# Cross-attention: the float32 quarter in every second head only, the other last quarters split by VectorE

## The chip, the cores and the metric

The kernel runs on one core of a Trainium2 chip. The metric is device time in microseconds, from one launch of the whole program; lower is better.

## The reference

The program is a two-layer block over x (4 x 512 x 512, float32) with a context of 4 x 1024 x 512: a gated masked cross-attention, a top-1 mixture of eight ternary experts, a second gated cross-attention with 16 heads, and a dense expert layer. The change lies in the second cross-attention alone:

```python
Q = query @ Wq.T + bq                      # 4 x 512 x 512, 16 heads of 32
K = key_value @ Wk.T + bk                  # 4 x 1024 x 512
V = key_value @ Wv.T + bv
scores = jnp.einsum('bhsd,bhtd->bhst', Q, K) * scale
attn = jax.nn.softmax(scores, axis=-1)     # over 1024 keys
ctx = jnp.einsum('bhst,bhtd->bhsd', attn, V)
return ctx @ Wo.T + bo
```

## The kernel before, in words

The phases run one after the other: context, readout, router, mixture, queries, **attention** (`attention_phase`, about 729 to 1180 us of the profile), output, experts. Attention walks over 64 heads (4 batches of 16), and each head over four quarters u = 0 to 3 of its 1024 keys, so there are 256 steps (h, u). Float32 accuracy comes from pairs of bf16 numbers: a high half and a low half.

In step (h, u) each engine does, in the order in which its queue is written:

- **TensorE** (PE): at one step in sixteen `max_transpose` (L1903); then `max_scores` (L1894) for the quarter of queries 28 steps ahead, four matmuls into one of two places of psM; then `scores` (L1916), four matmuls for the quarter of keys four steps ahead, into psE; then `mix` for the current quarter, into psO. The mix of quarters 0 to 2 is six bf16 matmuls (L1930): three products of the halves of the weights (the high half is read in place as the upper 16 bits of the float32 exponential, `upper`) and of the values, on two sides of the array at once. The mix of quarter 3 (`FULL = (3,)`) takes the float32 exponentials and float32 values directly: two float32 matmuls (L1935), which stand in the trace as four records.
- **VectorE** (DVE): `halves` for the quarter three steps ahead (L1819; only quarter 0 of the last seven heads), then `maximum` (L1811), the reduction of the psM place that the max_scores of this step fill; at u = 1 of every fourth head `next_values` joins the two halves of the next batch's values to float32 (L1603, `t_v`). At a few places it does odd work (bias split, sums and their reciprocal L1852 and L1854 at head 56).
- **ScalarE** (ACT): two exponentials (L1773) from psE into a ring of eight float32 quarters `t_e32`, four steps ahead; after quarter 3 the copy of psO (L1787).
- **GpSimd** (POOL): `halves` for the quarter four steps ahead: low = e32 - upper(e32) (L1726, `t_low`) for quarters 0 to 2; at one step in sixteen four small operations on the maxima (`max_parts`, L1736 to L1742).
- **SyncE** issues the loads and stores.

`wait_free` sets when max_scores may write a place of psM: the reduction of the max_scores two places before must be done. The transposed rows (L1903) take a place of their own in step (2, 1) of each group of four heads, so the max_scores that follow them there wait for the reduction of the step directly before, that of step (2, 0). The low halves lie in six slots, three for even and three for odd heads.

```python
for _, h, u in steps(b):                       # VectorE
    b2, h2, u2 = ahead(b, h, u, AHEAD - 1)
    if within(b2, h2):
        halves(b2, h2, u2)
    b2, h2, u2 = ahead(b, h, u, EARLY)
    if within(b2, h2):
        maximum(b2, h2, u2)
    prepare_output(b, h, u)
    if u == 1:
        next_values(b * NH + h - G - 3)
```

Of the kernel before, what the change touches and what calls it, by code (L numbers as in the profile page):

```python
# [7 lines left out]
BF16 = mybir.dt.bfloat16  # L8
# [4 lines left out]
P = 128  # L13
B, S, D = 4, 512, 512
T = 1024
KC = D // P
NH, HD = 16, 32
# [1494 lines left out]
def attention_phase(nc, queries_dram, keys_dram, values_dram, mixed_dram, sums_dram, ident, qst, loaded, kst, vst, kv_loaded, ones_set, o):  # L1512
# [7 lines left out]
    G = HG  # L1520
    TC = T // P
    AHEAD, MAXAHEAD = 4, 7
    RING = 8
    FULL = (3,)
    SIDE = P // 2
    NLD = 3
    mixed_v = mixed_dram.rearrange("b r (h d) s -> b h r d s", h=NH)
# [2 lines left out]
    with ExitStack() as c:  # L1530
        sb = lambda name, shape, dt: c.enter_context(nc.sbuf_tensor(name, shape, dt))
        sem = lambda name: c.enter_context(nc.semaphore(name))
        e32 = sb("t_e32", [P, RING, 2, S], F32)
        low = sb("t_low", [P, RING - 2 * len(FULL), 2, S], BF16)
        v32 = sb("t_v32", [P, G, TC, VW * G], F32)
        nmax = sb("t_nmax", [P, 2, G, 4], F32)
        nrest = sb("t_nrest", [P, G, 4], F32)
# [21 lines left out]
        mixed, mix_cleared, sums_added = sem("t_mixed"), sem("t_mix_cleared"), sem("t_sums_added")  # L1559
        copied_out = sem("t_copied_out")  # L1560
        stored = [sem(f"t_stored{i}") for i in range(2)]

        def on_pool(head, u):

            return u not in FULL and not on_dve(head, u)

        def on_dve(head, u):

            return u == 0 and head >= B * NH - MAXAHEAD

        def upto(chosen, head, u):

# [2 lines left out]
        def wait_lo(eng, head, u):  # L1575

            if on_pool(head, u):
                eng.wait_ge(lo_pool, upto(on_pool, head, u))
            else:
                eng.wait_ge(lo_dve, upto(on_dve, head, u))  # L1580

        def slot(h, u):

            return (h * 4 + u) % RING

        def low_slot(h, u):

            return h % 2 * (4 - len(FULL)) + u

        def upper(h, u):  # L1590

            return e32[:, slot(h, u), :, :].rearrange("p i s -> p (i s)").bitcast(BF16).rearrange(
                "p (i s w) -> p i s w", i=2, w=2)[:, :, :, 1]

        def ahead(b, h, u, n):

            h, u = h + (u + n) // 4, (u + n) % 4
            return b + h // NH, h % NH, u

        def join_values(engine, b, g):  # L1600

            halves = [vst[:, g, :, r * VW * G:r * VW * G + P] for r in range(2)]
            return engine.tensor_tensor(v32[:, g, :, 0:P], halves[0], halves[1], ALU.add).then_inc(v32_ready[g], 1)  # L1603

        def steps(b):
            return [(b, h, u) for h in range(NH) for u in range(4)]
# [7 lines left out]
        def within(b, h):  # L1614

            return not (isinstance(b, int) and b > LAST)
# [30 lines left out]
        def group_at(b, h, u, step):  # L1647

            if (4 * h + u) % GROUP == step:
                b2, h2, _ = ahead(b, h // G * G, 0, GROUP)  # L1650
                if within(b2, h2):
                    return b2, h2 // G
            return None

        with nc.Block() as block:
# [64 lines left out]
            @block.gpsimd  # L1720
            def _(pool):
                def halves(b, h, u):
                    head = b * NH + h
                    if on_pool(head, u):
                        pool.wait_ge(expd, head * 8 + 2 * u + 2)
                        nc.gpsimd.tensor_tensor(low[:, low_slot(h, u), :, :], e32[:, slot(h, u), :, :], upper(h, u),  # L1726
                                                ALU.subtract).then_inc(lo_pool, 1)

                def max_parts(b, g):

                    k = b * G + g
                    pool.wait_ge(maxed, k * GROUP + GROUP)
                    if not (isinstance(b, int) and b == 0 and g == 0):
                        pool.wait_ge(n_xposed, k)
                    m, zeros = nmax[:, g % 2, :, :], nparts[:, 3, :, :]
                    nc.gpsimd.tensor_tensor(nparts[:, 0, :, :], m, zeros, ALU.subtract).then_inc(n1_done, 1)  # L1736
                    pool.wait_ge(n1_done, k + 1)
                    nc.gpsimd.tensor_tensor(nrest[:, :, :], m, nparts[:, 0, :, :], ALU.subtract).then_inc(nrest_done, 1)
                    pool.wait_ge(nrest_done, k + 1)
                    nc.gpsimd.tensor_tensor(nparts[:, 1, :, :], nrest[:, :, :], zeros, ALU.subtract).then_inc(n2_done, 1)  # L1740
                    pool.wait_ge(n2_done, k + 1)
                    nc.gpsimd.tensor_tensor(nparts[:, 2, :, :], nrest[:, :, :], nparts[:, 1, :, :],  # L1742
                                            ALU.subtract).then_inc(n3_done, 1)

                nc.gpsimd.memset(nparts[:, :, :, :], 0.0).then_inc(zeros_set, 1)
                pool.wait_ge(zeros_set, 1)
                nc.gpsimd.memset(o.bones[:, :], 1.0).then_inc(o.bones_set, 1)
                pool.wait_ge(zeros_set, 1)
                nc.gpsimd.memset(v32[:, :, :, P:], 1.0).then_inc(v32_ones, 1)
                for g in range(G):  # L1750
                    pool.wait_ge(kv_loaded[g], 16 * KV_LOADS)
                    join_values(nc.gpsimd, 0, g)
                max_parts(0, 0)
                for n in range(AHEAD):
                    halves(*ahead(0, 0, 0, n))
                def batch(b):
                    for _, h, u in steps(b):
                        b2, h2, u2 = ahead(b, h, u, AHEAD)
                        if within(b2, h2):
                            halves(b2, h2, u2)  # L1760
                        if due := group_at(b, h, u, SPLIT_AT):
                            max_parts(*due)
                for b in range(B):
                    batch(b)
# [42 lines left out]
            def _(dve):  # L1807
# [7 lines left out]
                def halves(b, h, u):  # L1815
                    head = b * NH + h
                    if on_dve(head, u):
                        dve.wait_ge(expd, head * 8 + 2 * u + 2)
                        nc.vector.tensor_tensor(low[:, low_slot(h, u), :, :], e32[:, slot(h, u), :, :], upper(h, u),  # L1819
                                                ALU.subtract).then_inc(lo_dve, 1)  # L1820

                nc.vector.memset(psO[:, :, :], 0.0).then_inc(mix_cleared, 1)
                for m in range(EARLY):
                    maximum(*ahead(0, 0, 0, m))
                    if m >= EARLY - AHEAD + 1:
                        halves(*ahead(0, 0, 0, m - EARLY + AHEAD - 1))
# [56 lines left out]
            def _(pe):  # L1883
# [36 lines left out]
                def mix(b, h, u):  # L1920

                    head = b * NH + h
                    g = h // G
                    high, whole = upper(h, u), e32[:, slot(h, u), :, :]

                    def values(i, r):
                        return vst[:, g, 2 * u + i, r * VW * G:(r + 1) * VW * G].rearrange("p (w h) -> p h w", h=G)[:, h % G, :]

                    def add(side, i, r, part, first=False, last=False):
                        return nc.tensor.matmul(psO[side * SIDE:side * SIDE + VW, h % 2, :], values(i, r), part[:, i, :],  # L1930
                                                start=first, stop=last)

                    def add_whole(i, last):
                        v = v32[:, g, 2 * u + i, :].rearrange("p (w h) -> p h w", h=G)[:, h % G, :]
                        return nc.tensor.matmul(psO[i * SIDE:i * SIDE + VW, h % 2, :], v, whole[:, i, :], start=False, stop=last)  # L1935

                    if u in FULL:
                        pe.wait_ge(expd, head * 8 + 2 * u + 2)
                        if h % G == 0:
                            pe.wait_ge(v32_ready[g], b + 1)  # L1940
                        add_whole(0, u == 3)
                        add_whole(1, u == 3).then_inc(mixed, 1)
                        return
                    if u == 0:
                        pe.wait_ge(copied_out, head + 1)
                    rest = low[:, low_slot(h, u), :, :]
                    wait_lo(pe, head, u)
                    add(0, 0, 0, high, first=u == 0)
                    add(1, 0, 0, rest, first=u == 0)
                    add(0, 1, 0, high)  # L1950
                    add(1, 1, 0, rest)
                    add(0, 0, 1, high, last=u == 3)
                    add(1, 1, 1, high, last=u == 3).then_inc(mixed, 1)
# [627 lines left out]
```

## Time and profile before

| what | value |
|---|---|
| median of 3 runs | 1642.63 us (1638.8 to 1645.27) |
| the profiled execution's own time | 1641.37 us |
| its span | 1639.6 us |
| granted TensorE clock, mean over the span | 0.922 |
| busy over the span: PE, DVE, ACT, POOL | 86%, 69%, 58%, 32% |
| busy in 800 to 900 us, inside attention: PE, DVE, ACT, POOL | 99.8, 82.7, 75.3, 93.6 us of 100 |
| L1726, GpSimd's subtraction | 185 times, 2.0 us in the mean |
| L1811, VectorE's reduction | 256 times, 1.22 us |

The shares over the whole span mix phases with different limits; the row of 800 to 900 us is what bears on the change. Times are microseconds unless marked ns. PE is the matmul side of TensorE, PEld its weight loads, which overlap it. A line of the timeline gives start, duration (of the whole run of instructions where several are merged, marked x2, x3 and so on), engine, line, operation and tiles, and in brackets the idle time before it with what ended it. The clock is a share of 2.4 GHz; the chip grants either all or half of it.

### The profile page before, as it was taken

To read this page: it belongs to the slowest core of one execution; us is meant where nothing else is said; L and a number is where in the kernel's file an instruction comes from. 1 tells how busy PE (TensorE), PEld (TensorE's weight loads), DVE (VectorE), ACT (ScalarE), POOL (GpSimd) and SP (SyncE) were. 2 spreads that over 40 slices of the span, in tenths; PEclk is the share of its full clock that TensorE was granted. 3 is DMA by queue.
4 is the path that set the end of the run, shared out by engine and by line. 5 is a ranking of instruction groups with operands and counts; after the bars stand their busy time and mean duration, and the time that the engine had idled before them with its cause. 6 is when DMAs were issued, how large, how long until landed. Compare 5 with 4: busy or idle time off the path is not lost. (4 is left out here: it accounts for less than half of the span.)

```text
span 1639.6 us, 26673 instructions
## 1 busy us (share of the span) xinstructions
PE 1409.4 (86%) x9883; PEld 851.5 (52%) x9959; DVE 1132.4 (69%) x1444; ACT 950.4 (58%) x1440; POOL 524.4 (32%) x401
## 2 busy tenths in 40 slices
PE   4999996999942794779999999999795899999996
PEld 3555453555422352323776776775233666666663
DVE  4788856578873596838778788786576676565561
ACT  5788843445433595423777777777623866665651
POOL 0122210000053005314999999997520000000000
PEclk8999998999965896876999999999897899999998
DMA  6688761000028438430353443542481876656640
GB/s 232 222 288 305 249 218 40 1 1 1 1 81 342 136 125 204 107 90 4 67 105 85 86 98 71 104 113 81 99 287 52 295 255 231 207 204 211 220 145 27
DMA packets 162674, 233.22 MB, mean 142 GB/s; under 512 B 46396, under 2 KB 80191, under 8 KB 161416
## 3 DMA queue, kind: packets, MB, share of 16 engines
q1 hardware_dynamic: 157064, 206.60, 41.8%
q0 software_dynamic: 5504, 25.20, 4.2%
q8 instruction: 67, 1.10, 0.3%
q14 instruction: 39, 0.32, 0.1%
HBM read 169.62 MB, written 55.65 MB: 137 GB/s over the span
## 5 line engine op out<-in xcount | busy, mean ns | idle before, releaser
L1726 POOL TENSOR_TENSOR t_low<-t_e 128x1024 bf16<-128x1024 f32 x185 | 365.0, 2001 | 48.1 <-ACT t_e L1773 48.1
L1811 DVE TENSOR_REDUCE t_nmax<-t_psM 128x1 f32<-128x1024 f32 x256 | 309.5, 1221 | 75.0 <-PE t_psM L1894 73.6
L1773 ACT ACTIVATE t_e<-t_psE 128x512 f32<-128x512 f32 x512 | 277.9, 595 | 105.0 <-PE t_psE L1916 97.5
L1894 PE MATMUL t_psM<-kst,qst 96*64 96x512 bf16 x1024 | 189.0, 406 | 14.0 <-DVE t_nmax L1811 7.0
L2411 PE MATMUL e_psG<-late_flat,e_w1p 128*128 (+1 forms) x1536 | 172.3, 275 | 13.7 <-DVE e_hT L2355 9.1
L1916 PE MATMUL t_psE<-qst,kst 99*64 99x512 bf16 x1024 | 181.9, 386 | 1.3
L2411 PEld LDWEIGHTS e_psG<-late_flat,e_w1p 128*128 128x128 bf16 x1536 | 151.3, 99 | 35.2 <-issue 8.3
L1930 PE MATMUL t_psO<-t_e,vst 128*33 128x512 bf16 x768 | 163.9, 392 | 3.7 <-POOL t_low L1726 3.7
L2426 PE MATMUL e_psO<-e_w2p,e_hT 128*128 128x512 bf16 x752 | 164.9, 379 | 0.8
L1894 PEld LDWEIGHTS t_psM<-kst,qst 96*64 96x64 bf16 x1024 | 89.0, 113 | 77.8 <-DVE t_nmax L1811 35.0
L2426 PEld LDWEIGHTS e_psO<-e_w2p,e_hT 128*128 128x128 bf16 x768 | 75.0, 98 | 89.0
L1930 PE MATMUL t_psO<-t_low,vst 128*33 128x512 bf16 x384 | 115.0, 380 | 0.0
L1916 PEld LDWEIGHTS t_psE<-qst,kst 99*64 99x64 bf16 x1024 | 80.6, 108 | 58.9 <-ACT t_e L1773 44.7
L116 POOL DMA_DIRECT2D ternary<-c_wout x48 | 42.5, 886 | 179.9 <-ACT c_wout L228 179.9
L2307 ACT CAST e_w2p<-xres 128x2048 bf16<-128x2048 f32 x32 | 60.7, 1898 | 52.7 <-PE e_psO L2426 27.2
L2313 ACT ACTIVATE e_g<-e_psG,e_b1T 128x256 f32<-128x256 f32 x128 | 53.5, 469 | 64.0 <-PE e_psG L2411 36.8
L1930 PEld LDWEIGHTS t_psO<-t_e,vst 128*33 128x33 bf16 x768 | 76.5, 109 | 23.7 <-POOL t_low L1726 4.7
L675 PE MATMUL a_psS<-ctxT,a_xT 128*128 128x512 bf16 x373 | 86.4, 386 | 0.7 <-issue 0.2
L358 PE MATMUL c_psG<-ctxT,c_wT 128*128 128x512 bf16 x369 | 85.7, 379 | 0.8
L361 PE MATMUL c_psG<-c_wT,ctxT 128*128 128x512 bf16 x371 | 85.6, 379 | 0.7
L2347 DVE TENSOR_TENSOR e_w1p<-piece,e_w1p 128x2048 bf16<-128x2048 f32 x32 | 72.2, 2287 | 18.2 <-ACT e_w1p L2302 18.2
L2355 DVE TENSOR_TENSOR e_hT<-e_g,e_hT 128x512 bf16<-128x512 f32 x64 | 43.7, 689 | 51.0 <-ACT e_hT L2316 51.0
(268 smaller groups left out, 2376.4 us busy)
## 6 DMA issues: line engine op xcount, KB each, us to landing
piece<-in_L_ffn_w SPq DMA_DIRECT2D x32, 1024.0 KB, 13.8
xres<-in_L_ffn_w SPq DMA_DIRECT2D x32, 1024.0 KB, 14.8
wT<-ternary POOLq DMA_DIRECT2D x8, 1536.0 KB
kst<-keys SPq DMA_DIRECT2D x96, 128.0 KB, 3.5
c_rows<-in_ctx SPq DMA_DIRECT2D x8, 1024.0 KB, 9.4
xres<-in_L_ffn_wg SPq DMA_DIRECT2D x8, 1024.0 KB, 6.1
xres<-in_L_ffn_wu SPq DMA_DIRECT2D x8, 1024.0 KB, 6.8
xres<-in_L_ffn_wd SPq DMA_DIRECT2D x8, 1024.0 KB, 6.2
```

The source lines that it names most:

```text
L358: last = nc.tensor.matmul(psG[:, k, :], wT[:, 0, a, k * P:(k + 1) * P], ctxT[:, b, q * 512:(q + 1) * 512], start=(i == 0), stop=(i == 11))
L361: last = nc.tensor.matmul(psG[:, k, :], ctxT[:, a, q * 512 + k * P:q * 512 + (k + 1) * P], wT[:, 1, b, :], start=(i == 0), stop=(i == 11))
L675: last = nc.tensor.matmul(psS[:, par, h * 512:(h + 1) * 512], xT[:, par, ra * KC + k, :], ctxT[:, rb * KC + k, bass.ds(b * T + h * 512, 512)],
L1726: nc.gpsimd.tensor_tensor(low[:, low_slot(h, u), :, :], e32[:, slot(h, u), :, :], upper(h, u), ALU.subtract).then_inc(lo_pool, 1)
L1773: nc.scalar.activation(e32[:, slot(h, u), i, :], psE[:, i, :], ACT.Exp, scale=SC).then_inc(expd, 1)
L1811: nc.vector.tensor_reduce(nmax[:, h // G % 2, h % G, u:u + 1], banks_of(place_of_max(b, m)).rearrange("p a t -> p (a t)"), AX_X, ALU.max, ...
L1894: last = nc.tensor.matmul(banks_of(place_of_max(b, m))[side * SIDE:(side + 1) * SIDE, i, :], qst[0:KR, g, h % G, s0:s0 + SIDE], kst[0:KR, ...
L1916: last = nc.tensor.matmul(psE[side * SIDE:(side + 1) * SIDE, i, :], kst[:, g, h % G, t0:t0 + SIDE], qst[:, g, h % G, :], start=True, stop= ...
L1930: return nc.tensor.matmul(psO[side * SIDE:side * SIDE + VW, h % 2, :], values(i, r), part[:, i, :], start=first, stop=last)
L2347: nc.vector.tensor_tensor(half1(1, p), raw1(p), half1(0, p), ALU.subtract).then_inc(w1_lo, 1)
L2411: last = nc.tensor.matmul(psG[:, g % 4, i, :], w1p[:, ra, k, f:f + P], xeT[:, rb * KC + k, ee, :].rearrange("p o s -> p (o s)"), start=(n ...
L2426: last = nc.tensor.matmul(psO[:, m, :], hT[:, ra, k, m * P:(m + 1) * P], w2p[:, rb, k, :], start=(k == 0 and i == 0), stop=(k == FC - 1 an ...
```

## The change

In heads with an odd number the last quarter stays float32 (`is_whole`). In even heads it becomes a bf16 quarter like the other three: its low half is formed by VectorE (`on_dve`), in the VectorE step (h, 0) of the same head, ahead of that step's reduction. The low slots become one ring of six over the seven low quarters of each pair of heads, and each engine that forms a low half first waits until the mix that read the slot before is done (`wait_low_free`). TensorE's wait for the joined values moves from the first to the second head of each group of four. GpSimd still forms three low halves for each head.

```diff
-    FULL = (3,)
+    LOWS = 6
...
-        low = sb("t_low", [P, RING - 2 * len(FULL), 2, S], BF16)
+        low = sb("t_low", [P, LOWS, 2, S], BF16)
...
+        def is_whole(head, u):
+            return u == 3 and head % 2 == 1
+
         def on_pool(head, u):
-            return u not in FULL and not on_dve(head, u)
+            return not is_whole(head, u) and not on_dve(head, u)

         def on_dve(head, u):
-            return u == 0 and head >= B * NH - MAXAHEAD
+            return u == 3 and head % 2 == 0 or u == 0 and head >= B * NH - MAXAHEAD
+
+        def low_count(head, u):
+            return head // 2 * 7 + head % 2 * 4 + u
+
+        def wait_low_free(eng, head, u):
+            n = low_count(head, u) - LOWS
+            if n >= 0:
+                pair, quarter = divmod(n, 7)
+                eng.wait_ge(mixed, pair * 8 + quarter + 1 + RING)
...
-        def low_slot(h, u):
-            return h % 2 * (4 - len(FULL)) + u
+        def low_slot(head, u):
+            return low_count(head, u) % LOWS
...
                 def halves(b, h, u):                      # GpSimd; VectorE the same with on_dve
                     head = b * NH + h
                     if on_pool(head, u):
+                        wait_low_free(pool, head, u)
                         pool.wait_ge(expd, head * 8 + 2 * u + 2)
...
-                    if u in FULL:
+                    if is_whole(head, u):
                         pe.wait_ge(expd, head * 8 + 2 * u + 2)
-                        if h % G == 0:
+                        if h % G == 1:
                             pe.wait_ge(v32_ready[g], b + 1)
```

## Rows read from the trace of the kernel before

**Rows 1.** Busy time of each engine in one group of four heads.
```profile
core 0: us, PE busy (x) PEld busy (x) DVE busy (x) ACT busy (x) POOL busy (x), PEclk, DMA share, GB/s
921.21:947.21 26.00, 25.95 (x221) 18.59 (x218) 20.95 (x18) 19.64 (x38) 24.10 (x17) 1.00 0.43 88
```

**Rows 2.** Groups by line, 735 to 1230 us: busy, mean ns, idle before, releaser.
```profile
L1811 DVE TENSOR_REDUCE t_nmax<-t_psM 128x1 f32<-128x1024 f32 x252 | 304.8, 1221 | 73.7 <-PE t_psM L1894 72.4
...
L1935 PE MATMUL t_psO<-t_e,t_v 128*33 128x512 f32 x256 | 72.0, 598 | 0.0
...
L1603 DVE TENSOR_TENSOR t_v<-vst 128x1024 f32<-128x1024 bf16 x12 | 20.6, 1714 | 0.0
L1819 DVE TENSOR_TENSOR t_low<-t_e 128x1024 bf16<-128x1024 f32 x7 | 9.1, 1293 | 23.3 <-ACT t_e L1773 23.3
```

**Rows 3.** Timeline of TensorE, steps (1, 2) to (2, 1) of heads 20 to 23.
```profile
904.95 0.38 PE L1930 MATMUL t_psO<-t_low,vst 128*33 128x512 bf16 x1
...
905.61 0.75 PE L1894 MATMUL t_psM<-kst,qst 96*64 96x512 bf16 x4
...
906.51 1.15 PE L1935 MATMUL t_psO<-t_e,t_v 128*33 128x512 f32 x4
907.37 0.72 PE L1894 MATMUL t_psM<-kst,qst 96*64 96x512 bf16 x4
...
909.14 0.23 PE L1903 MATMUL t_psM<-ident,t_nparts 128*128 128x128 bf16 x1
909.42 0.62 PE L1894 MATMUL t_psM<-kst,qst 96*64 96x512 bf16 x4
```

**Rows 4.** Timeline of ScalarE, VectorE and GpSimd in the same steps.
```profile
906.69 1.08 ACT L1773 ACTIVATE t_e<-t_psE 128x512 f32<-128x512 f32 x2 [0.47 <-PE t_psE L1916]
...
908.14 1.22 DVE L1811 TENSOR_REDUCE t_nmax<-t_psM 128x1 f32<-128x1024 f32 x1 [0.50 <-PE t_psM L1894]
...
906.87 0.22 POOL L1736 TENSOR_TENSOR t_nparts<-t_nmax,t_nparts 128x16 bf16<-128x16 f32 x1
...
907.76 0.21 POOL L1742 TENSOR_TENSOR t_nparts<-t_nrest,t_nparts 128x16 bf16<-128x16 f32 x1
907.93 1.89 POOL L1726 TENSOR_TENSOR t_low<-t_e 128x1024 bf16<-128x1024 f32 x1
```

**Rows 5.** Timeline of all three around the join before head 24.
```profile
917.63 1.71 DVE L1603 TENSOR_TENSOR t_v<-vst 128x1024 f32<-128x1024 bf16 x1
...
919.26 1.21 DVE L1811 TENSOR_REDUCE t_nmax<-t_psM 128x1 f32<-128x1024 f32 x1
...
920.40 2.34 DVE L1811 TENSOR_REDUCE t_nmax<-t_psM 128x1 f32<-128x1024 f32 x2
...
916.37 1.89 POOL L1726 TENSOR_TENSOR t_low<-t_e 128x1024 bf16<-128x1024 f32 x1 [0.99 <-ACT t_e L1773]
...
918.22 2.87 POOL L1726 TENSOR_TENSOR t_low<-t_e 128x1024 bf16<-128x1024 f32 x1
...
921.05 1.89 POOL L1726 TENSOR_TENSOR t_low<-t_e 128x1024 bf16<-128x1024 f32 x1
...
922.91 1.89 POOL L1726 TENSOR_TENSOR t_low<-t_e 128x1024 bf16<-128x1024 f32 x1
...
918.81 0.75 PE L1894 MATMUL t_psM<-kst,qst 96*64 96x512 bf16 x4
...
920.56 0.73 PE L1894 MATMUL t_psM<-kst,qst 96*64 96x512 bf16 x4
...
923.66 0.59 PE L1894 MATMUL t_psM<-kst,qst 96*64 96x512 bf16 x3
```

**Rows 6.** Timeline of GpSimd, VectorE and TensorE at head 56.
```profile
1132.17 5.02 POOL L1726 TENSOR_TENSOR t_low<-t_e 128x1024 bf16<-128x1024 f32 x1 [2.37 <-ACT t_e L1773]
...
1134.29 1.15 DVE L1819 TENSOR_TENSOR t_low<-t_e 128x1024 bf16<-128x1024 f32 x1
1135.37 2.33 DVE L1811 TENSOR_REDUCE t_nmax<-t_psM 128x1 f32<-128x1024 f32 x2
...
1136.63 0.62 PE L1894 MATMUL t_psM<-kst,qst 96*64 96x512 bf16 x4 [3.27 <-DVE t_nmax L1811]
```

**Rows 7.** Busy time and granted clock of the 4 us after that stall.
```profile
1138.00:1142.00 4.00, 4.00 (x22) 1.48 (x20) 2.06 (x2) 2.69 (x6) 1.05 (x1) 0.57 0.21 51
```

More of the change, by code:

```diff
@@ L1724, in halves @@
                     if on_pool(head, u):
+                        wait_low_free(pool, head, u)
                         pool.wait_ge(expd, head * 8 + 2 * u + 2)
-                        nc.gpsimd.tensor_tensor(low[:, low_slot(h, u), :, :], e32[:, slot(h, u), :, :], upper(h, u),
+                        nc.gpsimd.tensor_tensor(low[:, low_slot(head, u), :, :], e32[:, slot(h, u), :, :], upper(h, u),
                                                 ALU.subtract).then_inc(lo_pool, 1)
@@ L1817, in halves @@
                     if on_dve(head, u):
+                        wait_low_free(dve, head, u)
                         dve.wait_ge(expd, head * 8 + 2 * u + 2)
-                        nc.vector.tensor_tensor(low[:, low_slot(h, u), :, :], e32[:, slot(h, u), :, :], upper(h, u),
+                        nc.vector.tensor_tensor(low[:, low_slot(head, u), :, :], e32[:, slot(h, u), :, :], upper(h, u),
                                                 ALU.subtract).then_inc(lo_dve, 1)
@@ L1945, in mix @@
                         pe.wait_ge(copied_out, head + 1)
-                    rest = low[:, low_slot(h, u), :, :]
+                    rest = low[:, low_slot(head, u), :, :]
                     wait_lo(pe, head, u)
```

## The prediction, made before the run

> **What bounds the kernel now.** I read the busy times by stretch first, then the groups of instructions by line, then the timeline of one group of four heads. In the stretch of four heads of [rows 1] TensorE is busy 25.95 of 26.00 us at full clock, GpSimd 24.10, VectorE 20.95, ScalarE 19.64. So TensorE sets the pace of attention, GpSimd is 1.9 us behind it, and a shorter TensorE step can be worth something. [Rows 3] show the steps from the start of one kind of matmul to the next: the mix of a bf16 quarter takes 904.95 to 905.61, 0.66 us, that of the float32 quarter 906.51 to 907.37, 0.86 us.
>
> "Busy" hides how little room the other engines have. TensorE's max_scores write two buffers of psM that VectorE must reduce before they are written again. As a rule that leaves two steps, but where the transposed rows (L1903) take one of the two places, the next max_scores waits for the reduction directly before it. [Rows 3, 4] show this: the reduction that starts at 908.14 ends at 909.36, and the max_scores start at 909.42. That is 0.06 us after it, with no room at all, once in every four heads.
>
> **What the change removes.** In 32 of 64 heads the float32 mix (0.86 us) becomes a bf16 mix (0.66 us): 32 x 0.20 = 6.4 us less on TensorE [rows 3]. The range of this term is 5 to 6.4 us, since ScalarE is nearly as slow as a bf16 step (a pair of exponentials plus its wait is 1.08 + 0.47 = 1.55 us, [rows 4]), and since the last heads are not paced by TensorE.
>
> **What it adds.** 32 subtractions on VectorE. The same instruction stands in the trace seven times, near the end, at 1.29 us in the mean [rows 2]; back to back the next VectorE instruction starts 1.08 us after it (1134.29 to 1135.37, [rows 6]). In VectorE's queue the subtraction for quarter 3 of an even head h stands in step (h, 0), right in front of the reduction of that step. So not VectorE's total matters (20.95 + 2 x 1.3 = 23.6 of 26), but how late that one reduction becomes. Nothing is added to GpSimd's own count (three a head, as before); its new wait for a free low slot is for a mix of six or seven quarters earlier, while the exponentials that it waits for anyway come out at most four quarters ahead of the mix. So it costs nothing, and the ring of six is no limit.
>
> **The port.** [Rows 5] show what a VectorE instruction with two SBUF inputs and a GpSimd subtraction do to each other. The join of the values is issued at 917.63, while GpSimd works until its next one starts at 918.22. VectorE's next instruction starts at 919.26, so the join held something for 1.04 us after 918.22 and had waited 0.59 before. GpSimd's subtraction of 918.22 takes 2.87 us and not 1.89: it stood still for 0.98. In [rows 6] a GpSimd subtraction that starts at 1132.17 takes 5.02 us, over a reciprocal and the added subtraction after it: VectorE got its second turn though GpSimd was waiting. I take it that each added subtraction waits for the GpSimd instruction under way, is then next, and takes 1.05 us from both.
>
> The Trainium skill states this rule (SBUF — State Buffer, "Who interferes with whom"): a VectorE instruction with two SBUF inputs and a GpSimd instruction that reads SBUF exclude each other, and the second to issue blocks fully until the first is done. That speaks against this change, as the added work is of just that kind; the join's row agrees, and without the rule the forecast would be the third rival below.
>
> GpSimd's budget by this: 12 x 1.85 (918.22 would follow 916.37 by 1.85) + 1.06 for the maxima's parts (906.87 to 907.93, [rows 4]) + 0.98 for the join = 24.2 us in four heads; with two blocks of 1 us, 26.2. That is just over the old period of 26.0 and under the period that comes out below, so it does not bind.
>
> **Heads 2, 6, ... 54 (14 times), step (2, 0).** The exponentials of quarter 3 end at 907.77 (906.69 + 1.08, [rows 4]), so the subtraction is ready at 907.84. GpSimd is then in the last small part (from 907.76), and its next large one starts at 907.93. VectorE goes first: 907.93 + 1.05 = 908.98 is the start of the reduction, + 1.22 = 910.20 its end, + 0.06 = 910.26 the max_scores, which started at 909.42. Stall 0.84 us; 14 x 0.84 = 11.8 us. The margin to GpSimd's start at 907.93 is only 0.09 us: were GpSimd first, the stall would be 1.85 more.
>
> **Heads 0, 4, ... 56, step (0, 0).** In [rows 5] VectorE comes out of the join late: its last reduction before the step starts at 920.40 and the next thing could start at 921.53. The exponentials are there by then (0.40 after the max_scores of 920.56, as 907.77 after 907.37). GpSimd is in the subtraction that started at 921.05 and hands over at 922.91. The added subtraction holds until 923.96, the reduction ends at 925.17, and the max_scores of step (0, 2), now at 923.66, start at 925.23. Stall 1.57 us, at 12 heads (12 joins, [rows 2]): 18.8 us. Where no join precedes (heads 0, 4 and 56), GpSimd is 0.98 earlier and hands over at 921.93: reduction ended 924.19, stall 0.6. At head 56 the sums and the reciprocal follow this reduction, and the whole delay of 0.65 + 1 adds to the stall that is there [rows 6]: 1.6. Together 0.6 + 0.6 + 1.6 = 2.8 us.
>
> In the new frame GpSimd still idles about 1 us before quarter (2, 0) and 0.6 before (0, 0), so it starts each pair on time, and these phases repeat in each group.
>
> **Sum.** 11.8 + 18.8 + 2.8 - 6.4 = +27.0 us. The profiled execution took 1641.37 us, which gives 1668.4; from the median of the runs, 1642.63, it is 1669.6. I say 1670. In four heads: 26.0 - 0.4 + 0.84 + 1.57 = 28.0 us.
>
> Bounds of the added stalls: from below nothing (only -6.4 us, 1636); from above, if GpSimd is first at the 14 close places, 14 x 1.85 = 26 us more, 1696.
>
> **Rivals.**
> A. *The subtraction is hidden* and the change does what it takes off TensorE: 1642.6 - 6.4 = 1636. For it: the join, 1.71 us of VectorE, moved TensorE by nothing; the step behind it is 1.75 us (918.81 to 920.56, [rows 5]) as it is elsewhere (905.61 to 907.37, [rows 3]). Against it: the reduction two steps on ended at 920.47 and the max_scores started at 920.56 [rows 5], so the join uses up all the room, and at 909.42 there was none. It decides if VectorE gets to the subtraction over 1.2 us before the reduction's data. Chance 0.04.
> B. *GpSimd first at the close places*: the stall of 0.84 becomes 2.69. 1696. For it: a margin of 0.09 us. Against: VectorE got the turn at both contested places of rows 5 and 6. Chance 0.13.
> C. *No exclusion at the port*, or GpSimd out of phase: then the subtraction costs only VectorE's time. At (2, 0): 907.84 + 1.13 + 1.22 + 0.06 = 910.25, stall 0.83; at (0, 0) after a join: 921.53 + 1.13 + 1.21 + 0.06 = 923.93, stall 0.27; at the others none but 1.1 at head 56. 11.6 + 3.2 + 1.1 - 6.4 = +9.5, 1652. Against: 2.87 and 5.02 us of rows 5 and 6. Chance 0.11.
> D. *The clock*: after the one long stall of TensorE (3.27 us before 1136.63, [rows 6]) the granted clock was 0.57 in the 4 us from 1138 [rows 7], that is mostly the 1.2 GHz level. If a stall of 1.6 us did that 12 times, some 3.4 us at half speed each cost 1.7: 12 x 1.7 = 20 us more, 1690. Against: the pause here is half as long. Chance 0.12.
> E. *GpSimd's budget or ScalarE's pace sets the period* and swallows the stalls: 26.2 to 26.5 us for four heads, 14 x 0.2 to 0.5 = +3 to +7, 1645 to 1650. Chance 0.06.
> The forecast has the rest, 0.54.
>
> **Numbers.** The forecast's own width is 1662 to 1678. The range has to reach to D and, below, nearly to C: 1652 to 1692 leaves out A, B, E and part of C, about 2 in 10. This kernel's measurement tells 0.5%, 8.2 us, from no change. Faster by more than that hardly anything (A gives 6.4 us): 0.03. Within it: the rest of A, E, a little of C: 0.07. Slower: 0.90.
>
> **What the profile would show.** Right: PE idle before L1894, released by VectorE's L1811, about 0.8 us at the step after each L1903 and 1.6 us two steps into every fourth head; a group of four heads near 28.0 us; the added subtractions at 1.2 us where GpSimd is between instructions and up to 3 us where they wait; the float32 mix at 128 records and not 256 [rows 2], the mix of quarter 3 of even heads at 0.66. GpSimd's subtraction behind each added one at 2.9 us. Wrong: PE waits for t_low in the steady stretch (then GpSimd is the bound), a period under 26.2 us, a granted clock under 1.00 between 770 and 1130 us, or GpSimd's subtraction at 1.89 us beside the added one (then no exclusion).

## The result, and the profile after

The changed kernel takes 1678.9 us (median of 4 runs, 1676.78 to 1681.82), the kernel before, beside it, 1643.91 us. The ratio is 1.0224 (95% interval 1.0198 to 1.025), that is 35 us slower. The forecast was 1670 in a range of 1652 to 1692.

The page of the changed kernel, its busiest engines and the groups that bear on the change (busy, mean, idle before, releaser):

```profile
PE 1415.2 (84%) x10023; PEld 841.4 (50%) x10023; DVE 1192.4 (71%) x1476; ACT 948.0 (57%) x1440; POOL 552.7 (33%) x401
...
L1742 POOL TENSOR_TENSOR t_low<-t_e 128x1024 bf16<-128x1024 f32 x185 | 391.3, 2143 | 53.3 <-ACT t_e L1789 53.0
...
L1911 PE MATMUL t_psM<-kst,qst 96*64 96x512 bf16 x1024 | 184.1, 410 | 47.6 <-DVE t_nmax L1827 41.2
...
L1836 DVE TENSOR_TENSOR t_low<-t_e 128x1024 bf16<-128x1024 f32 x39 | 72.3, 1858 | 21.3 <-ACT t_e L1789 21.3
```

The same group of max_scores on the page of before:

```profile
L1894 PE MATMUL t_psM<-kst,qst 96*64 96x512 bf16 x1024 | 189.0, 406 | 14.0 <-DVE t_nmax L1811 7.0
```

Read the idle column. TensorE's max_scores (L1911) now wait 41.2 us for VectorE's reduction, where the page of before had 7.0. The 39 subtractions on VectorE take 1.86 us in the mean, where seven took 1.29 [rows 2]. GpSimd has the same 185 subtractions, at 2.14 us instead of 2.00.

A group of four heads in the steady stretch (busy time of each engine, as [rows 1]):

```profile
937.73:965.77 28.04, 25.76 (x224) 17.87 (x221) 24.43 (x20) 19.53 (x38) 26.08 (x17) 1.00 0.41 82
```

28.04 us, forecast 28.0. TensorE is now idle 2.3 us in it. The two places of that idle time are in the timeline. Step (2, 1), which answers to [rows 3] and [rows 4]:

```profile
951.64 1.27 DVE L1836 TENSOR_TENSOR t_low<-t_e 128x1024 bf16<-128x1024 f32 x1 [0.24 <-ACT t_e L1789]
952.83 1.21 DVE L1827 TENSOR_REDUCE t_nmax<-t_psM 128x1 f32<-128x1024 f32 x1
...
951.61 0.22 POOL L1758 TENSOR_TENSOR t_nparts<-t_nrest,t_nparts 128x16 bf16<-128x16 f32 x1
951.78 2.87 POOL L1742 TENSOR_TENSOR t_low<-t_e 128x1024 bf16<-128x1024 f32 x1
...
952.90 0.23 PE L1920 MATMUL t_psM<-ident,t_nparts 128*128 128x128 bf16 x1
954.09 0.62 PE L1911 MATMUL t_psM<-kst,qst 96*64 96x512 bf16 x4 [0.96 <-DVE t_nmax L1827]
```

VectorE's subtraction is issued at 951.64, 0.14 us ahead of GpSimd's at 951.78, and GpSimd's takes 2.87 us. The reduction ends at 954.04 and the max_scores start at 954.09. They come 1.19 us after the transposed rows, where [rows 3] have 0.28: a stall of 0.91 us, forecast 0.84.

Steps (0, 0) to (0, 2), which answer to [rows 5]:

```profile
936.92 1.21 DVE L1827 TENSOR_REDUCE t_nmax<-t_psM 128x1 f32<-128x1024 f32 x1
938.05 2.50 DVE L1836 TENSOR_TENSOR t_low<-t_e 128x1024 bf16<-128x1024 f32 x1
940.47 1.21 DVE L1827 TENSOR_REDUCE t_nmax<-t_psM 128x1 f32<-128x1024 f32 x1
...
937.58 1.89 POOL L1742 TENSOR_TENSOR t_low<-t_e 128x1024 bf16<-128x1024 f32 x1
...
939.43 2.87 POOL L1742 TENSOR_TENSOR t_low<-t_e 128x1024 bf16<-128x1024 f32 x1
...
938.61 0.69 PE L1911 MATMUL t_psM<-kst,qst 96*64 96x512 bf16 x4
...
941.74 0.62 PE L1911 MATMUL t_psM<-kst,qst 96*64 96x512 bf16 x4 [1.32 <-DVE t_nmax L1827]
```

Here GpSimd was first (937.58). The subtraction is issued at 938.05, waits until GpSimd's boundary at 939.43 and ends at 940.55; the reduction ends at 941.68. From max_scores to max_scores there are 3.13 us, where [rows 5] have 1.55 in the mean of two steps (920.56 to 923.66): a stall of 1.6 us, forecast 1.57.

One place came out as rival B had it. At head 2, in the first group, GpSimd was first by 0.13 us:

```profile
780.38 2.85 DVE L1836 TENSOR_TENSOR t_low<-t_e 128x1024 bf16<-128x1024 f32 x1 [0.52 <-ACT t_e L1789]
783.15 1.21 DVE L1827 TENSOR_REDUCE t_nmax<-t_psM 128x1 f32<-128x1024 f32 x1
...
780.25 1.89 POOL L1742 TENSOR_TENSOR t_low<-t_e 128x1024 bf16<-128x1024 f32 x1
...
784.41 1.02 PE L1911 MATMUL t_psM<-kst,qst 96*64 96x512 bf16 x4 [2.81 <-DVE t_nmax L1827]
...
784.00:788.00 4.00, 3.59 (x18) 1.53 (x20) 1.58 (x2) 1.09 (x2) 1.79 (x2) 0.57 0.17 22
```

TensorE waits 2.81 us. In the window of 784 to 788 us (last line, busy time and granted clock), which begins with the last 0.41 us of that wait, the clock is 0.57.

### The profile page after: what moved, and what is told of

Same layout as the page of the kernel before. It is cut to its first block and busy times, and to the rows that moved or that the text cites. A ratio compares the mean times of both kernels' runs of the same rounds, so it can differ in the third digit from the quotient of the medians.

```text
span 1675.2 us, 27127 instructions
## 1 busy us (share of the span) xinstructions
PE 1415.2 (84%) x10023; PEld 841.4 (50%) x10023; DVE 1192.4 (71%) x1476; ACT 948.0 (57%) x1440; POOL 552.7 (33%) x401
## 3 DMA queue, kind: packets, MB, share of 16 engines
q1 hardware_dynamic: 157064, 206.60, 41.2%
## 5 line engine op out<-in xcount | busy, mean ns | idle before, releaser
L1742 POOL TENSOR_TENSOR t_low<-t_e 128x1024 bf16<-128x1024 f32 x185 | 391.3, 2143 | 53.3 <-ACT t_e L1789 53.0
L1911 PE MATMUL t_psM<-kst,qst 96*64 96x512 bf16 x1024 | 184.1, 410 | 47.6 <-DVE t_nmax L1827 41.2
L1947 PE MATMUL t_psO<-t_e,vst 128*33 128x512 bf16 x896 | 192.0, 393 | 2.5 <-POOL t_low L1742 2.5
L1933 PE MATMUL t_psE<-qst,kst 99*64 99x512 bf16 x1024 | 176.1, 387 | 1.2
L1911 PEld LDWEIGHTS t_psM<-kst,qst 96*64 96x64 bf16 x1024 | 82.1, 113 | 109.5 <-DVE t_nmax L1827 77.3
L1947 PE MATMUL t_psO<-t_low,vst 128*33 128x512 bf16 x448 | 135.0, 382 | 0.0
L1933 PEld LDWEIGHTS t_psE<-qst,kst 99*64 99x64 bf16 x1024 | 74.7, 109 | 62.5 <-ACT t_e L1789 44.9
L1947 PEld LDWEIGHTS t_psO<-t_e,vst 128*33 128x33 bf16 x896 | 87.5, 109 | 27.9 <-POOL t_low L1742 3.0
L1836 DVE TENSOR_TENSOR t_low<-t_e 128x1024 bf16<-128x1024 f32 x39 | 72.3, 1858 | 21.3 <-ACT t_e L1789 21.3
```

Source lines behind the costliest of these rows:

```text
L1742: nc.gpsimd.tensor_tensor(low[:, low_slot(head, u), :, :], e32[:, slot(h, u), :, :], upper(h, u), ALU.subtract).then_inc(lo_pool, 1)
L1911: last = nc.tensor.matmul(banks_of(place_of_max(b, m))[side * SIDE:(side + 1) * SIDE, i, :], qst[0:KR, g, h % G, s0:s0 + SIDE], kst[0:KR, ...
L1933: last = nc.tensor.matmul(psE[side * SIDE:(side + 1) * SIDE, i, :], kst[:, g, h % G, t0:t0 + SIDE], qst[:, g, h % G, :], start=True, stop= ...
```

## The experiments

Ten kernels, each the changed kernel with a small edit. The period is the time of one steady group of four heads in the stretch of 925 to 1125 us of its profile, from the first mix of one group to that of the next; it repeats to 0.05 us in every run but run 6. The whole time also holds up to 8 us by which the unchanged phases ahead of attention differ from one profiled execution to another (attention starts at 725.4 us in run 6, at 726.5 in before, at 733.0 in run 5), so differences of a few us are read from the period and from attention alone.

| run | edit | period, us | ratio to before |
|---|---|---|---|
| before | | 25.98 | 1 |
| the change | | 28.04 | 1.0224 (1.0198 to 1.025) |
| 1 | mix only, ring cleared first | 25.64 | 1.0019 (1.0002 to 1.0035) |
| 5 | mix only, ring cleared later | 25.64 | 0.9979 (0.9964 to 0.9995) |
| 2 | one SBUF input | 26.71 | 1.0104 (1.0076 to 1.0132) |
| 3 | reduction first | 26.22 | 1.0069 (1.0044 to 1.0093) |
| 4 | memset ahead of the subtraction | 28.16 | 1.0202 (1.017 to 1.0233) |
| 6 | GpSimd first | 31.4 to 32.8 | 1.0494 (1.0471 to 1.0517) |
| 10 | no join | 27.07 | 1.0121 (1.0084 to 1.0158) |
| 7 | one in four | 25.86 | 1.0015 (0.9997 to 1.0034) |
| 8 | two, and one of GpSimd's | 26.14 | 1.0051 (1.0033 to 1.0068) |
| 9 | one in four, steady groups only | 25.88 | 1.0002 (0.9988 to 1.0017) |

**Runs 1 and 5, what the mix gives.**

```diff
         def on_dve(head, u):
-            return u == 3 and head % 2 == 0 or u == 0 and head >= B * NH - MAXAHEAD
+            return u == 0 and head >= B * NH - MAXAHEAD
...
-                    wait_lo(pe, head, u)
+                    if u == 3:
+                        pe.wait_ge(expd, head * 8 + 2 * u + 2)
+                    else:
+                        wait_lo(pe, head, u)
```

> Leaves out the subtraction for the last quarter of even heads (its low slot holds what an earlier quarter left); TensorE's part of the change stays. It prices the gain alone. My theory (TensorE sets the pace, 0.20 us less for each of 32 quarters): 6 us under the kernel before (5 to 7), 25.6 us for four heads. A rival in which ScalarE or GpSimd sets the period once TensorE is faster: 0 to 3 us under before, 25.8 us or more for four heads, and ScalarE or t_low named in front of TensorE's matmuls.

> As the first run (no subtraction for the last quarter of even heads, its low half left out), but the clearing of the low ring, which held up the first max_scores there, now stands behind GpSimd's joins, where GpSimd is idle. Theory: the group of four heads stays at 25.64 us as in the first run and attention starts as early as in the kernel before, so the whole is 3 to 5 us under before. Rival (the gain inside attention is given back later): within 1 us of before.

The period falls by 0.34 us, 0.17 for each quarter, not 0.20. What holds the rest, no run tells apart. Run 1 as a whole was no faster: its clearing of the ring stood on GpSimd in front of the small memset of t_v (L1768) that lets the first max_scores start, and TensorE's wait there is 10.21 us for 5.80 in before:

```profile
728.57 5.22 POOL L1762 MEMSET t_low<- 128x6144 bf16 x1 [34.10 <-POOLq L1313]
...
734.66 0.64 PE L1914 MATMUL t_psM<-kst,qst 96*64 96x512 bf16 x2 [10.21 <-POOL t_v L1768]
```

With the clearing moved, run 5 is 0.21% under before (medians of 1641.4 and 1643.9 us). That is all that there was to win, and it is under the 0.5% of the forecast's measure. It is also less than the periods promise. In the profiles the first fourteen groups take 4.8 us less than in before, but the last two give 1.6 us back. In them the stall at head 56 is 3.27 us as before, and the 1.2 GHz level after it lasts 6.8 us for 3.4.

**Run 2, the second SBUF input taken away.**

```diff
+                        if u == 3:
+                            nc.vector.tensor_reduce(waste[:, :], e32[:, slot(h, u), :, :].rearrange("p i s -> p (i s)"),
+                                                    AX_X, ALU.max).then_inc(lo_dve, 1)
+                            return
```

> As the changed kernel, but the added VectorE instruction for the last quarter of even heads is a reduction of the same 1024 float32 elements (one SBUF input, 1.2 us, same place in the queue, same semaphore), and the low half is left out. It keeps VectorE's time and takes the second SBUF input away. Theory (the port is exclusive): GpSimd's subtractions behind it go back from 2.87 to 1.89 us, the stall in step (2, 0) stays at 0.8 us (there VectorE hardly waits), the one in step (0, 0) falls from 1.6 to about 0.3 us; in all 8 to 14 us over before. Rival (only VectorE's queue order matters, the port does not): the same time as the changed kernel, 32 to 36 us over before.

From the groups by line (735 to 1250 us) and the timeline of VectorE at step (0, 0):

```profile
L1744 POOL TENSOR_TENSOR t_low<-t_e 128x1024 bf16<-128x1024 f32 x185 | 365.9, 2003 | 59.2 <-ACT t_e L1793 58.1 <-PE t_psO L1955 1.1
...
L1841 DVE TENSOR_REDUCE t_waste<-t_e 128x1 f32<-128x1024 f32 x32 | 38.8, 1214 | 12.5 <-ACT t_e L1793 12.5
...
933.12 1.20 DVE L1841 TENSOR_REDUCE t_waste<-t_e 128x1 f32<-128x1024 f32 x1
```

GpSimd's subtraction is back at 2.00 us and VectorE's extra instruction takes 1.20 to 1.22 us everywhere. The period is 26.71 us: (28.04 - 26.71) = 1.33 us of the 2.40 that the subtractions cost (28.04 - 25.64) come from the two engines' holding each other up, nearly all at head 0, and 1.07 from VectorE's time alone (forecast in rival C: 0.83 + 0.27 = 1.10). The whole was 16 us over before and not 8 to 14: it carries run 1's clearing of the ring, which holds up the start by 4.4 us. The rival is out. One reservation: the reduction writes one column and not 1024, so this run takes away the large SBUF write of the subtraction along with its second input, and does not tell the two apart.

**Run 3, the reduction first.**

```diff
-                        b2, h2, u2 = ahead(b, h, u, AHEAD - 1)
-                        if within(b2, h2):
-                            halves(b2, h2, u2)
                         b2, h2, u2 = ahead(b, h, u, EARLY)
                         if within(b2, h2):
                             maximum(b2, h2, u2)
+                        b2, h2, u2 = ahead(b, h, u, AHEAD - 1)
+                        if within(b2, h2):
+                            halves(b2, h2, u2)
```

> As the changed kernel, but in each VectorE step the reduction comes first and the subtraction after it. Theory (the one late reduction in front of max_scores is the cost): the 0.8 us stall at head 2 of each group is gone, and the one at head 0 too, since the subtraction finds GpSimd's next boundary 0.25 us later and the next reduction still has a step of room; what stays is GpSimd's budget, 24.2 + 2 x 1.0 = 26.2 us for four heads against 26.0 before: 0 to 8 us over before. Rival (VectorE's or GpSimd's total is what binds, wherever the subtraction stands): 25 us or more over before, TensorE waiting for t_low or for the reductions as in the changed kernel.

The same work in the same step, one place further back in VectorE's queue, takes 1.8 us less for four heads: 26.22 for 28.04. Both stalls are gone. So it was not the amount of VectorE's work but the one late reduction. The 26.22 agree with GpSimd's budget of 26.2, and I first took that for the reason; run 8 shows below that it is not. The whole is 10 us over before, not 0 to 8: at heads 18 and 20 the split of the output bias, one partition wide, stands behind the subtraction in the same step and takes 2.37 us instead of 1.09 and 0.82 in before, with about 4 and 3 us lost in those two groups. TensorE waits 2.63 and 1.90 us there, and 3.4 us at 1.2 GHz follow each time.

**Runs 4 and 6, who is first.**

```diff
                         dve.wait_ge(expd, head * 8 + 2 * u + 2)
+                        if u == 3 and head % 4 == 2:
+                            nc.vector.memset(waste[:, :], 0.0)
```

> As the changed kernel, with a memset of 200 columns on VectorE (about 0.25 us) between the wait and the subtraction at heads 2, 6, 10 and so on, so that GpSimd's next subtraction starts first. Theory (a lock taken at instruction boundaries, 0.14 us decide): the added subtraction takes about 2.9 us there instead of 1.27, the stall before max_scores grows from 0.84 to about 2.7 us at 13 more places, 24 us over the changed kernel; and if the pause lowers TensorE's clock as it did once at head 2, another 1.5 us each, so 24 to 44 us over the changed kernel. Rival (ports shared, no order of arrival): only the memset's own time, 14 x 0.25 = 3.5 us.

This one did not do what it was made for:

```profile
952.05 0.23 DVE L1838 MEMSET t_waste<- 128x200 f32 x1 [0.31 <-ACT t_e L1790]
952.19 1.16 DVE L1839 TENSOR_TENSOR t_low<-t_e 128x1024 bf16<-128x1024 f32 x1
...
952.12 2.98 POOL L1743 TENSOR_TENSOR t_low<-t_e 128x1024 bf16<-128x1024 f32 x1
```

GpSimd's subtraction starts at 952.12, ahead of VectorE's at 952.19, and still it is GpSimd's that is held (2.98 us). Its lead is only 0.07 us here, and 0.07 to 0.09 at twelve of the places from head 6 to head 54 (at head 18 VectorE was ahead); with 0.13 us GpSimd went first (head 2 above, run 6 below). The memset itself does not seem to need what GpSimd holds: at head 2 of this run it took 0.23 us as elsewhere (from 780.21) beside a GpSimd subtraction that ran from 780.01. Nor does a busy VectorE keep its turn for its next instruction as a rule: in the changed kernel GpSimd's 937.58 started while VectorE was in a reduction, and VectorE's next, at 938.05, waited. No run here tells the short lead from the memset in front as the reason.

[Rows 6] are another case: there a subtraction behind a reciprocal went ahead of a GpSimd instruction that had waited two microseconds. It is so in the nine traces that have the subtraction there; in runs 3 and 8, where a reduction stands behind the reciprocal, a GpSimd subtraction issued 0.08 us after the reciprocal took its usual 1.89 us beside it. Why GpSimd waited in the nine stays open. Run 6 therefore delays VectorE by a wait and not by work:

```diff
+                        if u == 3 and head % 4 == 2 and head < 56:
+                            dve.wait_ge(n3_done, head // 4 + 2)
                         dve.wait_ge(expd, head * 8 + 2 * u + 2)
```

> As the changed kernel, but at heads 2, 6 to 54 VectorE's subtraction also waits for the fourth small part on GpSimd, so that it is issued some 0.1 us behind GpSimd's next subtraction instead of 0.14 us ahead of it. Nothing else moves. Theory (whoever issues first while VectorE is idle has the port for the whole instruction): the subtraction takes 2.8 to 3.0 us there instead of 1.27, the stall grows by 1.85 us at 13 places, group period 29.9 us instead of 28.04, 24 us over the changed kernel; with a lowered clock behind each stall of 2.8 us, as once at head 2, up to 38 us over. Rival (VectorE always wins a contested port at once, or the port is shared in time): as the changed kernel, within 3 us.

```profile
996.10 2.84 DVE L1838 TENSOR_TENSOR t_low<-t_e 128x1024 bf16<-128x1024 f32 x1 [0.49 <-POOL t_nparts L1758]
998.86 1.21 DVE L1827 TENSOR_REDUCE t_nmax<-t_psM 128x1 f32<-128x1024 f32 x1
...
995.97 4.72 POOL L1742 TENSOR_TENSOR t_low<-t_e 128x1024 bf16<-128x1024 f32 x2
...
1000.12 1.06 PE L1913 MATMUL t_psM<-kst,qst 96*64 96x512 bf16 x4 [2.79 <-DVE t_nmax L1827]
...
999.00:1006.00 7.00, 5.88 (x28) 2.37 (x30) 3.52 (x3) 2.17 (x4) 3.65 (x3) 0.53 0.09 21
```

Now GpSimd is ahead by 0.13 us (995.97 against 996.10), the subtraction takes 2.84 us and TensorE waits 2.79. The kernel takes 1724.3 us, 45 us over the changed one, for a wait that moved one instruction by about 0.25 us (0.49 us idle before it, 0.24 in the changed kernel). The theory's 24 us are there and more than the 38 with the clock: the last line shows the granted clock at 0.53 over the 7 us after this stall. In the profile of this run the 1.2 GHz level follows each of the 12 such stalls from head 6 on (at head 18 the order was the other one, and TensorE's wait 1.2 us), for 3.4 or 6.8 us.

**Run 10, without the join.**

```diff
                         if u == 1:
-                            next_values(b * NH + h - G - 3)
+                            pass
```

> As the changed kernel, but VectorE never joins the next batch's values: the float32 quarters of batches 1 to 3 use batch 0's values. Theory (at heads 8, 12 to 52 the subtraction meets a VectorE and a GpSimd that the join has made 1 us late): the step that is 3.15 us there falls to the 2.21 us that it is at heads 4 and 56, the one at head 2 of each group stays at 2.97, period 27.1 us, 11 to 12 us under the changed kernel. Rival (the stall at head 0 has nothing to do with the join): the same time as the changed kernel.

The period is 27.07 us (forecast 27.1), and the stall before the max_scores at head 0 is down from 1.32 to 0.35 us of idle TensorE:

```profile
931.28 2.05 DVE L1836 TENSOR_TENSOR t_low<-t_e 128x1024 bf16<-128x1024 f32 x1 [0.24 <-ACT t_e L1789]
...
934.52 0.62 PE L1911 MATMUL t_psM<-kst,qst 96*64 96x512 bf16 x4 [0.35 <-DVE t_nmax L1827]
```

In all 16.8 us under the changed kernel by the medians, where 11 to 12 were expected. 12 x 0.97 = 11.6 of it is the period. In the profiled executions attention is 12.8 us shorter in all (the group of head 56 gives 1.1) and the whole 13.4; the rest of the 16.8 is the spread of four runs (1660.4 to 1668.9).

**Runs 7 to 9, is there a version that wins?**

```diff
         def is_whole(head, u):                        # run 7
-            return u == 3 and head % 2 == 1
+            return u == 3 and head % 4 != 2 and head < B * NH - MAXAHEAD
...
         def on_dve(head, u):                          # run 8, on top of every second head
+            return u == 3 and not is_whole(head, u) or u == 0 and (head % 4 == 2 or head >= B * NH - MAXAHEAD)
...
-                    if (b, u) == (1, 0) and 1 <= h < 6:
+                    if (b, u) == (1, 2) and 1 <= h < 6:
```

> A mend: the last quarter is bf16 with VectorE's subtraction only at head 2 of each group of four and in the last seven heads, VectorE's reduction goes ahead of the subtraction, and the bias split of batch 1 moves from u = 0 to u = 2. Theory: GpSimd has 24.2 + 1.0 = 25.2 us of work for four heads, TensorE 26.0 - 0.17 = 25.8, so TensorE sets the period: 25.8 us, 2 to 3 us less over the steady groups, 1 to 2 us less in the last heads, 3 to 5 us under before in all. Rival (any subtraction on VectorE costs more than the 0.17 us that the mix gives): 0 to 5 us over before.

> The last quarter bf16 in every second head as in the change, but VectorE's reduction goes first, the bias split is at u = 2, the last seven heads are all bf16, and VectorE also takes quarter 0 of head 2 of each group from GpSimd. Theory of GpSimd's budget: 24.2 + 3 x 1.0 - 1.85 = 25.4 us, under TensorE's 25.64, so the period falls from the 26.22 of the run with the reduction first to 25.7, 4 to 6 us under before in all. Rival (VectorE with three subtractions at 1.05 us and up to 1.85 us of waiting each is now late for its reductions): a period of 26 to 27 us, TensorE waiting for the reductions, 0 to 15 us over before.

> As the run with one bf16 quarter in four heads, but the last eight heads are as in the kernel before (float32 last quarter), only the added subtraction stands behind the reduction, and the bias split is at u = 3. Theory: what that run lost, it lost at heads 16 to 20 (0.9 us more) and in the last heads and the gap behind attention (4 us more); without them the steady groups' 0.12 us each remain: 1.5 to 2 us under before, 25.86 us for four heads, the gap between attention's last copy and the output phase back at 2.8 us. Rival: the gain stays lost somewhere, no difference from before or slower.

Run 7 has the period that was forecast for it, 25.86, and no gain as a whole. At heads 56 to 59 its group takes 29.3 us for 27.12, and VectorE, with seven more subtractions in the last heads, ends the quotients of the first batches late, so that the output phase starts 7 us after attention's last copy and not 2.8:

```profile
1185.81 2.29 DVE L1894 TENSOR_TENSOR late_flat<-late_flat,t_v 128x2048 f32<-128x2048 f32 x1
1189.21 1.42 DVE L2118 SCALAR_TENSOR_TENSOR o_cpair<-late_flat,o_bias,o_cpair 128x512 bf16<-128x512 f32 x2 [1.11 <-ACT o_cpair L2081]
```

In the profile of before these quotients end at 1182.3, 1.6 us after the last copy. Run 9 leaves the last heads alone (27.13 and 22.26 us for the last two groups, as before) and is level with before: 10 groups at 0.1 us less are 1 us, and the groups of heads 16 and 20, with the bias split, give 1.2 us back.

Run 8 takes 1.85 us from GpSimd and gives it one more block. Its budget is then 25.4 us, and the period only falls from 26.22 to 26.14. So in run 3 GpSimd's budget was not the bound. What both have in common is VectorE at the join, here in run 3:

```profile
951.26 2.29 DVE L1618 TENSOR_TENSOR t_v<-vst 128x1024 f32<-128x1024 bf16 x1
```

It takes 2.29 us, where it takes 1.71 in [rows 5], since GpSimd's instruction had begun 0.68 us before it and not 1.26. The reductions behind it are late, and the step behind it, (3, 3), is 0.5 us longer in both runs (2.25 us for 1.75). No run here beats the kernel before clearly; without the added subtraction (run 5, which leaves the low half out) it would be 0.2%.

## Why the prediction was right

The place, the mechanism and the size held. In twelve groups, those of heads 8 to 52, the change costs 2.0 to 2.1 us each (head 20's 2.7), forecast 2.0. Runs 3 and 6 show that it is the lateness of one reduction, run 2 that the exclusion makes more than half of it (1.33 of 2.40 us for four heads), run 10 that the join sets the size at head 0.

Term by term, in the profiled execution (1676.95 - 1641.37 = 35.6 us slower, forecast 27.0):

- *Saving, 6.4 us*: too large. It is 0.17 and not 0.20 us for a quarter (runs 1 and 5), which would be 5.4 us for 32; but where it was measured as a whole, from the first mix to the last copy of run 5, 3.2 us are left of it, under the stated 5 to 6.4.
- *Step (2, 0), 0.84 us*: 0.91. But at head 2 GpSimd was first: the first group takes 30.9 us for 25.8, 5.1 us more where 1.0 was forecast. That is rival B at one place of 14, with rival D's clock behind it, and so one of the stated signs of being wrong, a granted clock under 1.00 between 770 and 1130 us, did appear (784.5 to 787.9). The margin that I called 0.09 us was 0.14 in the steady groups and the other way round in the first, whose exponentials run in another phase.
- *Step (0, 0), 1.57 us*: 1.6 behind a join. At heads 0 and 4, forecast 0.6, it is 1.05 and 0.65.
- *Head 56, 1.6 us*: the stall at the sums and the reciprocal is 4.44 us for 3.27 and the step before is 0.65 longer, but the lowered clock also lasts 6.8 us and not 3.4; that group is 2.8 us longer, not 1.2.
- *Last four heads*: 1.8 us less up to the start of the last mix, where 0.4 less was forecast.
- *Outside attention*, not in the forecast: 1.5 us ahead of it, in phases that the change doesn't touch, and 1.7 us behind it: the quotients on VectorE end later against the last copy.

Together the groups make 32.5 us and the rest 3.1. The misses hardly cancel: only the last four heads took less than forecast, and the 8.6 us between 27.0 and 35.6 are mostly the first group's 4.1 and the 3.1 outside. The largest miss is that I treated the 14 places of step (2, 0) as alike, though the first group has no steady phase.

Rival A is out (no room at all for VectorE's reduction in front of the transposed rows' successor), and so is C (2.87 us beside the added subtractions of the steady groups). D did not occur behind the stalls at head 0 that it was about: the clock stays at 1.00 through all of them. E did not occur.

The rule of the Trainium skill (SBUF — State Buffer, "Who interferes with whom") held in its main part: the second to issue blocks for the first's whole instruction, in both directions, as 951.64 against 951.78 and 780.38 against 780.25 show. What the rows add is how far ahead "first" has to be, by the start times of the profile: VectorE still won 0.07 to 0.09 us behind GpSimd (run 4, with a memset in front), and GpSimd won from 0.13 us on. In the traces of all runs VectorE issued such an instruction more than 0.1 us after a GpSimd subtraction that was still there about 350 times, and went ahead of it at ten: nine right behind the reciprocal of head 56, as in [rows 6], and one in run 8 (899.58).

## What to carry to other kernels

Before you move work to an engine that is "only 80% busy", find the instruction behind which it will be queued, and see how long the critical engine can wait for that one; here the answer was 0.00 us at one step in sixteen. Put such work behind, not in front of, what others wait for: one swap of two calls gave 25 of the 35 us back. And ask what it shares with its neighbour: beside a GpSimd that is 93% busy, an added VectorE instruction with two SBUF inputs nearly always meets one under way or holds up the next, and who is first by a tenth of a microsecond can be worth a stall of 2 us and the clock after it.

## What the runs showed of the hardware that was not expected

- A stall of TensorE of 2.8 us was followed by 3.4 to 6.8 us at 1.2 GHz (granted clock 0.57 and 0.53 above) though the engine had been busy for 10.00 of the 10 us up to 781 in the changed kernel; stalls of 0.96 and 1.32 us were not (1.00 throughout the steady groups). In between it went both ways: 1.90 us in run 3 was followed by 3.4 us at 1.2 GHz, 2.14 us in run 7 (before 1136.70) was not.
- A GpSimd subtraction that started 0.07 us ahead of VectorE's was the one that was held (2.98 us in run 4, VectorE's 1.16, with a memset in front of it); with a lead of 0.13 us it was VectorE's (2.84 us in run 6, GpSimd's 1.89).
- A GpSimd subtraction that was issued during VectorE's reciprocal, with a subtraction next in VectorE's queue, was held through both, 5.02 us in all [rows 6], and so in nine traces (4.49 to 5.82 us); with a reduction next, one issued at the reciprocal's start was not held (1.89 us, runs 3 and 8).
- A VectorE instruction on one partition and 512 columns took 2.37 us between two GpSimd subtractions (run 3, heads 18 and 20), three times its 0.82: a small instruction pays the whole wait.
